# Smaller patches for a deformable convolution: 14 by 8 pixels that serve two groups of four by four sample positions

## The reference, cut to what matters

```
x = relu(x)
offset = conv(x, w_off, padding 1) + b_off          # 18 channels: (dy, dx) for 9 taps
py = base_y + off[:, :, 0]; px = base_x + off[:, :, 1]
samp = bilinear_gather(x, py, px)                   # (B, C, 9, H, W)
out = einsum('bckhw,ock->bohw', samp, w_def)
```

## Time and profile before

| | |
|---|---|
| median of three runs | 1680.81 us (1674.68 to 1682.14) |
| the profiled execution's own time | 1692.53 us |
| its span, first to last instruction | 1690.7 us |
| mean granted TensorE clock | 0.962 of 2.4 GHz |
| TensorE busy | 1543.5 us, 91% |
| VectorE / ScalarE / GpSimd busy | 1096.4 / 990.7 / 941.8 us |

### The profile page before, as it was taken

One profiled execution on the slowest core, in us unless ns is written; L12 is line 12 of the kernel. 1 busy time (PEld: TensorE's weight loads), 2 busy tenths in 40 slices (PEclk: granted clock), 3 DMA queues, 4 the chain that ended last, 5 costly groups with the idle time before them and its releaser, 6 DMA issues.

```text
span 1690.7 us, 24883 instructions
## 1 busy us (share of the span) xinstructions
PE 1543.5 (91%) x8339; PEld 910.3 (54%) x8340; DVE 1096.4 (65%) x1964; ACT 990.7 (59%) x1564; POOL 941.8 (56%) x747
## 2 busy tenths in 40 slices
PE   6999999748998999989999999899999999889997
PEld 4777777514554555444554555455445554445554
DVE  6888888645666676565665666657556656556663
ACT  3555555435665666665666666557556666556662
POOL 4555555535565565555555655565556655556652
PEclk9999999858999999999999999999999999999999
DMA  5334333347777777777777777877787778777762
GB/s 149 116 117 116 116 115 112 120 145 250 235 253 247 244 259 236 235 230 236 244 230 240 237 256 246 235 239 240 238 249 247 267 230 247 219 235 251 253 243 68
DMA packets 145855, 356.90 MB, mean 211 GB/s; under 512 B 10875, under 2 KB 77976, under 8 KB 145752
## 3 DMA queue, kind: packets, MB, share of 16 engines
q1 hardware_dynamic: 131032, 328.46, 62.8%
q10 hardware_dynamic: 14720, 27.14, 4.6%
HBM read 292.42 MB, written 63.13 MB: 210 GB/s over the span
## 4 chain that ended last, share of the span: by engine, by line
DMA 42%; PE 23%; POOL 16%; issue 11%; DVE 3%; SPq 2%; ACT 1%; ACTq 0%; POOLq 0%; DVEq 0%
DMA hx_all<-hat_x 38%; POOL weights L1570 10%; PE bank L778 9%; PE pair L750 7%; POOL samples_hi L1519 4%; DMA hat_x<-hats 4%; PE pair L824 3%; SPq L564 2%; POOL rstd L1494 1%; PE pair L796 1%; POOL samples_lo L1506 1%; DVE hats L1299 1%; PE bank L796 1%; PE pair L762 1%; PE pair L764 1%
## 5 line engine op out<-in xcount | busy, mean ns | idle before, releaser
L1570 POOL TENSOR_TENSOR weights<-hy_all,hx_all 126x512 f32<-126x512 f32 x576 | 759.4, 1347 | 570.0 <-DMA hx_all<-hat_x 530.3
L1314 DVE SCALAR_TENSOR_TENSOR samples_lo<-bank,samples_hi 128x360 f16<-128x360 f32 (+1 forms) x832 | 434.1, 536 | 432.1 <-ACT samples_hi L1005 419.0
L778 PE MATMUL bank<-weights,zT 126*128 126x360 f32 (+1 forms) x1792 | 637.3, 474 | 78.1 <-POOL weights L1570 74.7
L1005 ACT ACTIVATE samples_hi<-bank 128x360 f16<-128x360 f32 (+1 forms) x832 | 385.4, 475 | 431.4 <-PE bank L778 405.0
L778 PEld LDWEIGHTS bank<-weights,zT 126*128 126x128 f32 x1792 | 314.8, 196 | 239.1 <-POOL weights L1570 79.7
L750 PE MATMUL pair<-samples_hi,w_hi 128*128 128x512 f16 x576 | 221.7, 385 | 1.3 <-DVE samples_lo L1314 1.3
L750 PE MATMUL pair<-samples_hi,w_lo 128*128 128x512 f16 x576 | 220.0, 382 | 0.0
L750 PE MATMUL pair<-samples_lo,w_hi 128*128 128x512 f16 x576 | 219.3, 381 | 0.0
L1506 POOL TENSOR_TENSOR samples_lo<-samples_hi,samples_lo 128x512 f16<-128x512 f32 x64 | 74.2, 1159 | 130.8 <-ACT samples_lo L909 130.7
L900 ACT ACTIVATE samples_hi<-pair,nbias,rstd 128x512 f32<-128x512 f32 x64 | 49.8, 778 | 148.5 <-PE pair L649 97.0
L948 ACT ACTIVATE z<-raw,norm_band 128x1764 f32<-128x1764 f32 (+3 forms) x80 | 132.1, 1671 | 0.0
(11 more groups left out here) (138 smaller groups left out, 1920.5 us busy)
## 6 DMA issues: line engine op xcount, KB each, us to landing
hy_all<-hat_y SPq DMA_DIRECT2D x192, 648.0 KB
hx_all<-hat_x SPq DMA_DIRECT2D x192, 648.0 KB
raw<-x_pad SPq DMA_DIRECT2D x68, 276.0 KB, 14.6
x_pad<-hy_all SPq DMA_DIRECT2D x64, 276.0 KB, 3.7
weights<-in_x SPq DMA_DIRECT2D x64, 256.0 KB, 3.0
out<-y SPq DMA_DIRECT2D x32, 512.0 KB, 13.5
hat_y<-hats ACTq DMA_DIRECT2D x64, 252.0 KB
hat_x<-hats ACTq DMA_DIRECT2D x64, 162.0 KB
```

The lines of the kernel that those rows point to most:

```text
L778: mm = nc.tensor.matmul(sampled_step(n, p)[:, :, c0 - first:c1 - first], zT[0:WPIX, u * WINDOWS + w, :], weights[0:WPIX, u, :, c0:c1], sta ...
L1005: nc.scalar.activation(samples_hi[:, u, :, c0:c1], sampled_step(n, p), ACT.Copy).then_inc(samples_ready, 1)
L1314: nc.vector.scalar_tensor_tensor(out=samples_lo[:, u, :, c0:c1], in0=sampled_step(n, p), scalar=1.0, in1=samples_hi[:, u, :, c0:c1], op0=A ...
L1570: nc.gpsimd.tensor_tensor(weights[0:WPIX, u, k, at:at + BW], hy_all[0:WPIX, k, :], hx_all[0:WPIX, k, :], ALU.mult).then_inc(weights_ready, 1)
```

## The change

The window becomes four columns by four rows (`WC = 4`, `HR = 4`), and a patch 14 rows by 8 columns, 112 pixels. One patch serves two groups of four by four positions, its upper and its lower half, so that a band has 18 "taps" (9 for each half) of 264 columns where it had 9 of 528. There are 17 windows and 16 steps of sampling, 288 columns each (the last 432). A hat in y now is loaded for `NEAR_R = 8` rows, where it was 12. The hats of a band are loaded in six pieces of 64 partitions x 768 floats, each for y and x, and `weigh` becomes six instructions of three taps, 112 x 768. The store of the hats moves from ScalarE's queue to SP's, behind `spread_hats`, and becomes six DMAs: y is stored twice (`COPIES = 2`), x once, each in two halves. The order list is written anew. The constant rows for the offsets (`ramps`) are loaded by eight more small DMAs, and the output is added in two parts for each band.

```diff
-BR, WC, UW = 8, 5, 64
+BR, WC, UW = 8, 4, 64
+HR = BR // 2
-CW = CENTERS * BR
+CW = CENTERS * HR
-WIN = WC * BR
+WIN = WC * HR
-NEAR_R = BR + 2 * REACH
+NEAR_R = HR + 2 * REACH
+COPIES = 2
-            "h0 s0 s1 s2 k0 h1 c0 c1 T0 k1 s3 s4 z0 z1 O0 k2 s5 s6 P0 c2 c3 T1 k3 s7 s8 c4 k4 c5 s9 Q0 "
-            "c6 k5 G0 T2 s10 k6 H0 c7 k7 s11 c8 T3 k8 s12 R0").split()]
+            "h0 s0 s1 s2 k0 h1 c0 c1 s3 s4 T0 k1 z0 z1 O0 s5 s6 P0 k2 c2 c3 s7 s8 T1 c4 k3 c5 s9 s10 "
+            "Q0 k4 c6 G0 T2 s11 s12 c7 k5 T3 s13 s14 c8 T4 s15 R0").split()]
...
-                for g in range(TROWS):
-                    wait(sp, weights_ready, TAPS * (n - 1) + TROWS * (g + 1))
-                    rows = [hat_rows[0][n % AHEAD, g, g:g + NEAR_R].rearrange("(r o) c -> r o c", o=1),
-                            hat_rows[1][n % AHEAD, g].rearrange("(o r) c -> o r c", o=1)]
-                    for dst, src in zip((hy_flat, hx_flat), rows):
-                        sp.dma_start(dst[g * SRC_C:(g + NEAR_R) * SRC_C,
-                                         g * CHUNK:(g + 1) * CHUNK],
-                                     src.broadcast_to([NEAR_R, SRC_C, CHUNK])
-                                     ).then_inc(hat_in[g], 16)
+                for i in range(PIECES):
+                    h, g = divmod(i, TROWS)
+                    wait(sp, weights_ready, PIECES * (n - 1) + i + 1)
+                    top = g + h * HR
+                    rows, columns = (slice(top * SRC_C, (top + NEAR_R) * SRC_C),
+                                     slice(i * CHUNK, (i + 1) * CHUNK))
+                    sp.dma_start(
+                        hy_flat[rows, columns],
+                        hat_y[n % AHEAD, g, top * COPIES:(top + NEAR_R) * COPIES, h]
+                        .rearrange("(a b) c -> a b c", b=1)
+                        .broadcast_to([COPIES * NEAR_R, SRC_C // COPIES, CHUNK])
+                    ).then_inc(hat_in[i], 16)
+                    sp.dma_start(
+                        hx_flat[rows, columns],
+                        hat_x[n % AHEAD, :, g, h].rearrange("(b a) c -> b a c", b=1)
+                        .broadcast_to([NEAR_R, SRC_C, CHUNK])).then_inc(hat_in[i], 16)
+
+            def store_hats(n):
+
+                sp.wait_ge(hats_ready, n + 1)
+                for h in range(2):
+                    columns = slice(h * HALF, (h + 1) * HALF)
+                    for copy in range(COPIES):
+                        sp.dma_start(
+                            hat_y[n % AHEAD].rearrange("g (r o) h c -> (g r) o h c", o=COPIES)
+                            [:, copy, h].rearrange("a (k c) -> a k c", k=TROWS),
+                            hats[0:Y_ROWS, 0, columns]).then_inc(hat_out[n % AHEAD], 16)
+                    sp.dma_start(
+                        hat_x[n % AHEAD].rearrange("r g h c -> (r g) h c")
+                        [:, h].rearrange("a (k c) -> a k c", k=TROWS),
+                        hats[0:X_ROWS, 1, columns]).then_inc(hat_out[n % AHEAD], 16)
...
                 if n + 2 < BANDS:
                     spread_hats(n + 2)
+                if n + AHEAD < BANDS:
+                    store_hats(n + AHEAD)
...
+                if p == STEPS - 1:
+                    pe.wait_ge(zT_a, zT_copied(n, TGROUPS - 1)[0])
...
-            def weigh(n, u, k):
-
-                if k % TROWS == 0:
-                    pool.wait_ge(hat_in[k // TROWS], 32 * n + 32)
-                if k == 0:
+            def weigh(n, u, i):
+
+                pool.wait_ge(hat_in[i], 32 * n + 32)
+                if i == 0:
                     wait(pool, sampled, STEPS * (n - 1))
...
+                nc.gpsimd.tensor_tensor(to, hy_all[0:WPIX, i * TROWS:(i + 1) * TROWS, :],
+                                        hx_all[0:WPIX, i * TROWS:(i + 1) * TROWS, :],
+                                        ALU.mult).then_inc(weights_ready, 1)
```

More of the change, by code:

```diff
@@ L306, in preact_conv_kernel @@
         hat_out = [sem(f"hat_out{s}") for s in range(AHEAD)]
-        hat_in = [sem(f"hat_in{g}") for g in range(TROWS)]
+        hat_in = [sem(f"hat_in{i}") for i in range(PIECES)]
         hats_ready = sem("hats_ready")
@@ L571, in _ @@
             sp.wait_ge(hats_cleared, 2)
-            spread_hats(0)
-            spread_hats(1)
+            for n in range(AHEAD):
+                store_hats(n)
+                if n + 1 < AHEAD:
+                    spread_hats(n)
             for n in range(BANDS + 2):
```

140 lines of the change are left out of this document (79 added, 61 removed).

## The result

The changed kernel takes 1659.49 us in the median (1659.32 to 1660.34, four runs) against 1679.61 (1674.68 to 1682.14, four runs) before: a ratio of 0.9885, interval 0.9861 to 0.9909. In these runs it is faster by 1.15%. I had forecast 1620: the sign was right and the outer range (1592 to 1665) held it, but the forecast's own range (1595 to 1645) did not, and the size was off by 40 us. The later runs do not bear the 1.15% out. In four later series the kernel before spread from 1591 to 1700 us (one disturbed execution left out), with medians of 1644, 1663, 1669 and 1675 us; over all 67 of these runs the median is 1662.7, and 32 of them were as fast as the changed kernel or faster. The changed one stayed at 1657 to 1661. So what is sure is that it varies less; its gain in the median depends on the runs that it is set beside.

A forecast was written before the change was run, and what follows sets the result against it. TensorE needs 18.9 us a band; the rest was waiting on DMA hat loads, and lost clock. 1692.5 − 91.8 − 3.8 + 37.8 − 8.2 + 0.5 = 1627.0 us, taken as 1620; range 1595 to 1645, outer 1592 to 1665.

The forecast's parts named there:

- The waits of 67 us and the clock's 24 us: In 59 bands: TensorE's 67.0 us waiting for GpSimd's `weights` and 24 us lost to its lowered clock, both taken as gone.
- The three terms forecast: VectorE, per band: 0.5 us for sampling copies, about 0.2 for the two-part output, at most 0.4 for a wider patch copy.
- rival 2: SP's queue becomes the limit, bands stay at 20.4 us, only the start is gained: 1675 us; chance 0.06.
- short rows: Hat loads: shorter rows cost more than their bytes, eight DMA engines bound from 1.32 times, about 1740 us at 1.5; chance 0.10.
- Rival 1: The copies behind sampling become the bound; at 1.4 us a band the median is about 1665 us; chance 0.14.
- the 0.6 forecast: TensorE's added time per band: 0.33 us of transposes, 0.2 at the band edge, 0.1 ahead of `locate`; range 0.33 to 1.4.
- `conv`, `locate` and the offsets stream what they did.: TensorE's work per band: these products stream the same columns as before, so no time was added for them.
- The start: Before the first sampling: smaller first hat loads and `weigh` without waits bring it earlier by 8 us (0 to 12).
- costed at nothing; up to +7 uncovered: Setup: eight more small constant loads take up to 0.9 us of SP each, 7 us in all, ahead of prefetched x loads.
- my step from 1627 to 1620: From profiled execution to median: the profiled one lay 11.7 us above its median; full transfer gives 1615, 1620 was taken.
- the 91.8 us: The 59 bands from 422.2 to 1629.1 us: their excess over 18.9 us each, waits and clock, removed in the sum.
- the wait ahead of s10: Ahead of `locate`: s10 waits for s7's copy, behind VectorE's offset split; +0.1 us a band (0 to 0.45).

The follow-up runs named there:

- late ramps: The changed kernel with the twelve small ramp loads spread over groups 2 to 4 of the first layer instead of ahead of its first x loads: 1653.17 us.
- the two gaps: Changed kernel, old offset read order, last transposes behind sampling, ramps later, GpSimd's pieces paired behind VectorE's z and offset splits: 1601.88 us (s10 behind `locate`), 1600.40 (s10 unmoved).

## Why the prediction was off

**Right, by its own steps.** The waits of 67 us and the clock's 24 us are gone. DMA is at 178 GB/s, 3.54 MB in 19.9 us, against 3.57 forecast. GpSimd's six pieces are at 11.6 us of busy time against 12.1. The copies are at 453 and 411 ns against 455 and 410. VectorE's busy time for a band was forecast at 13.9; it is 14.0 in the band shown, but 858.22 / 59 = 14.5 in the mean. The three terms forecast came to 1.0 us for 1.1; the rest is the offset split, 1.06 us longer, less the hats, 0.34 shorter, and I had neither. Neither SP's queue (rival 2) nor short rows (rival 3) bound anything. Rival 1, the late copies, holds in part: they cost 0.45 us a band at the edge.

**Right in size, taken together: transposes and edge.** The band without any of the causes is 19.00 us, 0.10 above the 18.90 of before, and the edge costs 0.45. Together that is 0.55 for the 0.6 forecast (0.33 of transposes, 0.2 of edge, 0.1 ahead of `locate`). How it divides is not shown. If the 18.90 holds an edge wait of 0.15, as at the edge of the earlier trace rows, the work grew by 0.25 and the edge by 0.30; but that row is of another edge, and the kernel before waited for `samples_lo` at 7 places in 59 bands only, by its product records.

**The step that failed** is one sentence of the sum over TensorE's work: "`conv`, `locate` and the offsets stream what they did." By columns they do. By time the eighteen offset products went from 402 to 451 ns each and from 2.06 to 2.49 us from start to start, since they now read their pixels in runs of four values in place of eight. The kernel's edit has this line; the diff shown ahead of the prediction leaves it out. The term was at nothing and measured 0.44 us a band, over the 61 passages that have these products 26.8 us. With it, 19.00 + 0.44 + 0.45 = 19.89, for the 19.92 measured.

The Trainium skill, "Advanced Engine Details and Errata", section "SBUF Cachelines", says that SBUF has 16-byte cachelines and that an access to a new one each time costs. Runs of eight 2-byte values, of four, and a row-wise read with a stepped write took 402, 451 and 630 ns here. The first two agree with it in direction; its section "PSUM Cachelines", which says that a non-contiguous pattern slows matmuls a lot, fits the third, where read and write changed together and were not told apart.

**The start** was missized by 7.05 us (−1.15 for −8.2). The term is "costed at nothing; up to +7 uncovered": the twelve small loads hold SP for 8.44 us, and with them out of the way 5.8 us came back. The remaining 1.2 may be the six stores, whose issuing takes 5 us ahead of the first load; with late ramps that load still goes out 2.0 us later than before, for the 1 us forecast. That part was not taken apart.

**The account.** The 63 passages took 1250.1 us (379.44 to 1629.5) where the sum had 1223.4: 26.7 more, for the offset products' 26.8; that the two meet so closely is in part luck, since the other terms were off by a tenth here and there. The start adds 7.05, the tail −0.45. 1627.0 + 33.3 = 1660.3, the profiled execution's time. The remaining 7 us are my step from 1627 to 1620. I took it because the profiled execution before lay 11.7 above its median; the likely reading is that this spread was the stalls' own, and so already in the 91.8 us that I removed.

**What I had not seen at all** is a price that another one covered. I had the split of the offsets at its mean of 1126 ns and the wait ahead of s10 at 0 to 0.45. The mean hid two lengths; two bands of the kernel before on VectorE, the first with GpSimd at rest, the second beside a running `weigh`:

```profile
572.16 0.69 DVE L1291 TENSOR_TENSOR offs_lo<-offs,offs_hi 114x512 f16<-114x512 f32 x1
```
```profile
591.24 1.64 DVE L1291 TENSOR_TENSOR offs_lo<-offs,offs_hi 114x512 f16<-114x512 f32 x1
```

The kernel before paid the long one in part of the bands; the change fills the pauses in which GpSimd waited for loads, so the split is long in every band shown here (2184 ns in the mean). It cost little only because the offset products had become 0.44 us longer. With those mended it costs 0.4 us a band: 1655.73 less 1631.45, over 61 bands.

## What to carry to other kernels

Where a change reorders the positions of a product, price the product by the pattern that it reads and writes, from a row with that pattern, and not by its columns. When a wait of one engine is removed, look at who ran undisturbed during it: a mean over two levels is the sign, and the shorter one may go away (`offs_lo`) or the longer one (`hats`, 1030 ns before and 694 after). Of two chains of equal length each hides the other, so an experiment that mends one alone shows nothing; mend both before calling a cause harmless. And before comparing medians, see whether the part that a change removes is the one that varies from run to run.

## What the hardware showed that I had not expected

Means on VectorE beside GpSimd's `weigh` and without it: `offs_lo` (two operands in SBUF) 2184 and 692 ns, `z_lo` 2257 and 846, `hats` (one operand, f32) 1680 and 694. `samples_lo`, with one operand in PSUM and one in SBUF, took 451 to 455 ns at 288 columns in all of these kernels. A piece of `weigh` itself was 1956 ns in the mean in the changed kernel and 1821 with the two gaps. How long the split is depends on where in a piece it begins: at the end of one 0.85 us, 0.23 us into one 2.29 us. The Trainium skill, "SBUF — State Buffer", section "SBUF: two separate sides", says that GpSimd and a VectorE operation with two SBUF inputs, or in a two-port mode, take a shared pair of ports by turns, each for a whole instruction, and that other VectorE work is not touched. The traces agree: 2184 − 692 = 1.49 us is less than one piece of `weigh`, the piece behind a split that came first took 2.49 us in place of 1.82, and `samples_lo` is untouched. That a port is what they share is the skill's account; the runs show only the turns.

Six DMA issues on ScalarE between two copies took 4.9 us once in a band and made one band 25.0 us where it was 19.9: TensorE's clock in that band was 0.90, and its products of 288 columns went from 414 to 467 ns in the mean. An issue has no fixed price: these take 0.8 us each, and the two of the kernel before, larger but of another form, took 0.31 and 0.34 us (one band):

```profile
1138.84 0.31 ACTq L997 DMA_DIRECT2D hat_y<-hats  x1
1139.19 0.34 ACTq L997 DMA_DIRECT2D hat_x<-hats  x1
```

That those two cost the kernel before nothing at their place was my assumption; no run here tested it.
